# Feed-forward in plain float32 matmuls, with W2 as the stationary operand and a transposed accumulator

## The reference

```
a = layernorm(x)                       # over the channels, eps 1e-6
q, k, v = a @ Wq, a @ Wk, a @ Wv       # 8 heads of 16
s = q k^T / 4 + time_bias + particle_bias, -inf where the key's time is later
x = x + softmax(s) v @ Wo
t = layernorm(x)                       # eps 1e-5
p = softmax(t @ Wg); top two of 8, made to sum to 1: top0, top1
for i in 0, 1:
    w_in = t * top_i
    out += sum over all 8 experts e of gelu(w_in @ W1[e] + b1[e]) @ W2[e]  + sum(b2)
x = x + out
```

## Time and profile before

| | |
|---|---|
| median of 3 runs | 2823.3 us (2819.64 to 2824.63) |
| span of the profiled execution | 2817.5 us, 5.8 us below the median of the runs; the profile gives no other time for this execution |
| mean granted TensorE clock | 0.965 of full speed |
| TensorE busy | 2460.9 us, 87% |
| ScalarE busy | 1694.7 us, 60% |
| VectorE busy | 1485.6 us, 53% |
| GpSimd busy | 1087.3 us, 39% |

### The profile page before, as it was taken

One profiled execution on the slowest core, in us unless ns is written; L12 is line 12 of the kernel. 1 busy time (PEld: TensorE's weight loads), 2 busy tenths in 40 slices (PEclk: granted clock), 3 DMA queues, 4 the chain that ended last, 5 costly groups with the idle time before them and its releaser, 6 DMA issues.

```text
span 2817.5 us, 57193 instructions
## 1 busy us (share of the span) xinstructions
PE 2460.9 (87%) x18611; PEld 2132.1 (76%) x18611; DVE 1485.6 (53%) x4157; ACT 1694.7 (60%) x2788; POOL 1087.3 (39%) x1054
## 2 busy tenths in 40 slices
PE   1658989899998989989899898989989898998989
PEld 0447778787877878877787777878877787877879
DVE  7545375445636554474554636544573555547454
ACT  2126666665665666556566665666566566656667
POOL 6014244343424434343343424333343433434337
PEclk9679999999999999999999999999999999999999
DMA  2412121030212203021030212103021120302100
GB/s 32 71 37 29 22 33 27 10 47 10 27 27 30 29 7 49 6 32 27 12 46 9 29 25 32 27 8 48 10 27 27 25 35 7 43 11 32 27 9 7
DMA packets 62290, 73.55 MB, mean 26 GB/s; under 512 B 15936, under 2 KB 43488, under 8 KB 61920
## 3 DMA queue, kind: packets, MB, share of 16 engines
q1 hardware_dynamic: 62016, 69.89, 17.1%
HBM read 11.19 MB, written 6.29 MB: 6 GB/s over the span
## 4 chain that ended last, share of the span: by engine, by line
PE 65%; DVE 12%; issue 10%; ACT 8%; DMA 2%; POOL 1%; SPq 1%; DVEq 0%; POOLq 0%; ACTq 0%
PE acc L912 17%; PE zps L901 8%; PE wide L819 7%; PE narrow L852 5%; PE wide L835 5%; ACT z L512 5%; PE zps L902 5%; PE zps L903 5%; PE wide L838 4%; PE wide L866 2%; PE wide L873 2%; DVE wide L664 1%; DVE h L735 1%; PE wide L859 1%; DMA stack<-halves 1%
## 5 line engine op out<-in xcount | busy, mean ns | idle before, releaser
L453 POOL TENSOR_TENSOR hsum<-h 128x384 f32<-128x384 f32 x1024 | 1027.6, 1007 | 1575.0 <-ACT h L541 1507.3
L540 ACT ACTIVATE h<-zps,b_col 128x384 f32<-128x384 f32 x1024 | 594.2, 580 | 751.6 <-DVE h L735 728.3
L735 DVE TENSOR_TENSOR h<-zps,ratio_b 128x384 f32<-128x384 f32 x1024 | 562.1, 554 | 910.1 <-PE zps L903 906.1
L912 PE MATMUL acc<-w,hsum 128*128 128x128 f32 x6144 | 863.0, 277 | 1.4 <-DVE outt L744 1.2
L912 PEld LDWEIGHTS acc<-w,hsum 128*128 128x128 f32 x6144 | 845.8, 194 | 2.2 <-POOL hsum L453 1.7
L541 ACT ACTIVATE h<-h,b_col 128x384 f32<-128x384 f32 x1024 | 620.4, 606 | 0.0
L901 PE MATMUL zps<-x_hi,w_lo 128*128 128x384 f32 x1024 | 449.8, 439 | 105.8 <-ACT h L540 64.0
L664 DVE CUSTOM_DVE_ANT_0 wide<-wide,query_table 128x768 f32<-128x768 f32 (+5 forms) x768 | 463.0, 651 | 123.1 <-PE wide L819 117.3
L835 PE MATMUL wide<-stack 128*128 128x256 f32 (+3 forms) x1280 | 364.7, 317 | 71.8 <-ACT z L512 33.6
L512 ACT ACTIVATE z<-wide 128x896 f32<-128x896 f32 (+2 forms) x384 | 344.8, 918 | 87.3 <-PE wide L838 86.8
L902 PE MATMUL zps<-x_lo,w_hi 128*128 128x384 f32 x1024 | 352.5, 344 | 0.0
(11 more groups left out here) (110 smaller groups left out, 1611.8 us busy)
## 6 DMA issues: line engine op xcount, KB each, us to landing
stack<-halves SPq DMA_DIRECT2D x512, 96.0 KB, 3.6
x_in<-in_x SPq DMA_DIRECT2D x136, 48.0 KB, 2.4
out_dram<-outt SPq DMA_DIRECT2D x256, 24.0 KB, 1.6
z<-in_L_ffn_W SPq DMA_DIRECT2D x8, 256.0 KB, 4.2
stack<-max_rows SPq DMA_DIRECT2D x64, 12.0 KB
bias_rows<-w_hi SPq DMA_DIRECT2D x1, 192.0 KB
bias_rows<-w SPq DMA_DIRECT2D x1, 192.0 KB
bias_rows<-w_lo SPq DMA_DIRECT2D x1, 192.0 KB
```

The costliest lines, as they stand in the source:

```text
L453: pool.tensor_tensor(hsum[:, m % NHS, :], h0[:, m % 2, :], h1[:, m % NH1, :], ALU.add).then_inc(hsum_ready, 1)
L540: act.activation(h0[:, m % 2, :], zps[m % 2][:, 0:CT], ACT.Gelu, bias=b1_col[:, j:j + 1]).then_inc(h0_ready, 1)
L735: vec.tensor_tensor(h1[:, m % NH1, :], zps[m % 2][:, 0:CT], ratio_b[:, c * CT:(c + 1) * CT], ALU.mult).then_inc(z1_ready, 1)
L912: ins = pe.matmul(acc[:, n * P:(n + 1) * P], hsum[:, k % NHS, n * P:(n + 1) * P], w2[:, j, :], start=(j == 0 and n == 0), stop=(j == UNITS ...
```

## The change

Layer one: W1 and x0 are kept whole in float32 (`w1`, `x0`), and a unit is one plain float32 matmul over 384 columns. The rounding and subtracting of W1 and of x0 go away; W1 is loaded straight to its place, right behind W2, during the first batch's attention. `x0` and `ratio_b` are two halves of one tile, which ScalarE fills with one copy per chunk.

Layer two: the W2 block is stationary and `hsum` moves, 384 columns in one matmul. The accumulator is then channels by tokens and has to be turned back: at the end of a chunk VectorE copies it to `acc_t`, TensorE transposes its three tiles into the same bank, and VectorE adds the residual as before. For chunk 0 the copy is in slot 31 and the transposes and the add in slot 33, for chunk 1 all is in slot 63 (`FINISH`). There are two accumulator banks, one for each chunk.

The second accumulator takes the bank of `narrow`. `mix` now writes both its parts into one wide buffer, and ScalarE copies 768 columns once, at the second part. `gate` writes to the free columns of the wide buffer that `turn` used, which is held until VectorE has taken the gate's maxima.

```diff
+FINISH = (33, UNITS - 1)
-WIDE = {(s, a): n for n, (s, a) in enumerate([(s, a) for _, s, a in PLAN if s in WIDE_STEPS])}
+WIDE = {(s, a): n for n, (s, a) in enumerate([(s, a) for _, s, a in PLAN if s in WIDE_STEPS and (s != "mix" or a[1])])}
+WIDE.update({("mix", (g, 0)): WIDE["mix", (g, 1)] for g in range(GROUPS)})
...
-        x0_hi = sb("x0_hi", [P, TOK], F32R)
-        x0_lo = sb("x0_lo", [P, TOK], F32R)
-        ratio_b = sb("ratio_b", [P, TOK])
+        x0_ratio = sb("x0_ratio", [P, 2, TOK])
+        x0, ratio_b = x0_ratio[:, 0], x0_ratio[:, 1]
+        acc_t = sb("acc_t", [P, CT])
...
-        acc = ps("acc", [P, 512])
-        narrow = ps("narrow", [P, 512])
+        acc = [ps("acc0", [P, 512]), ps("acc1", [P, 512])]
...
 SyncE, prepare
-                elif (step, a) == ("mix", (1, 1)):
-                    sp.wait_ge(narrow_filled, NARROW["mix", (1, 1)] + 1)
-                    for a in range(2):
-                        for e in range(4):
-                            sp.dma_start(z[:, a, e * DFF:(e + 1) * DFF], W1[4 * a + e]).then_inc(w1_loaded, 16)
+                    for e in range(EXPERTS):
+                        sp.dma_start(w1[:, e, :], W1[e]).then_inc(w1_loaded, 16)
...
 ScalarE, mix
-                elif step == "mix":
-                    cols = QCOLS if qc == 0 else TOK - QCOLS
-                    act.copy(mixed[:, qc * QCOLS:qc * QCOLS + cols], narrow[:, 0:cols]).then_inc(narrow_free, 1)
+                elif step == "mix" and a[1] == 1:
+                    act.copy(mixed[:, :], w[:, 0:TOK]).then_inc(wide_free[s], 1)
...
 ScalarE, split
-                    act.copy(x0_hi[:, a * CT:(a + 1) * CT], w[:, 0:CT]).then_inc(split_high, 1)
-                    act.copy(ratio_b[:, a * CT:(a + 1) * CT], w[:, 512:512 + CT]).then_inc(split_high, 1)
+                    act.copy(x0_ratio[:, :, a * CT:(a + 1) * CT],
+                             w[:, :].rearrange("p (k t) -> p k t", k=2)[:, :, 0:CT]).then_inc(wide_free[s], 1)
...
 VectorE, split
-                    vec.wait_ge(split_high, r.at(4, 2 * a + 2))
-                    ins = vec.tensor_tensor(x0_lo[:, a * CT:(a + 1) * CT], w[:, 0:CT], x0_hi[:, a * CT:(a + 1) * CT],
-                                            ALU.subtract)
-                    ins.then_inc(wide_free[s], 1)
...
 VectorE, after
                     vec.wait_ge(hsum_used, r.at(UNITS, k + 1 + NHS))
+                    vec.tensor_copy(acc_t[:, :], acc[c][:, 0:CT]).then_inc(acc_copied, 1)
+                if k in FINISH:
+                    c = FINISH.index(k)
+                    vec.wait_ge(out_turned, r.at(CHUNKS, c + 1))
                     vec.wait_ge(out_stored, r.at(16 * TPT * CHUNKS, 16 * (TPT * c + 1)))
                     vec.wait_ge(res_ready, r.at(CHUNKS, CHUNKS))
-                    vec.tensor_tensor(outt[:, :, :], acc[:, 0:CT].rearrange("p (i c) -> p i c", c=C),
+                    vec.tensor_tensor(outt[:, :, :], acc[c][:, 0:CT].rearrange("p (i c) -> p i c", c=C),
                                       res[:, c * HT:(c + 1) * HT, :], ALU.add).then_inc(out_ready, 1)
...
 TensorE, unit
-                pe.matmul(zp, lo, x0_hi[:, cols], start=True, stop=False)
-                pe.matmul(zp, hi, x0_lo[:, cols], start=False, stop=False)
-                pe.matmul(zp, hi, x0_hi[:, cols], start=False, stop=True).then_inc(z_filled, 1)
+                pe.matmul(zps[m % 2][:, 0:CT], w1[:, e, t * P:(t + 1) * P], x0[:, cols], start=True,
+                          stop=True).then_inc(z_filled, 1)
...
 TensorE, after
-                for n in range(HT):
-                    ins = pe.matmul(acc[:, n * P:(n + 1) * P], hsum[:, k % NHS, n * P:(n + 1) * P], w2[:, j, :],
-                                    start=(j == 0 and n == 0), stop=(j == UNITS_PER_CHUNK - 1), skip_group_check=True)
-                ins.then_inc(hsum_used, 1)
+                pe.matmul(acc[c][:, 0:CT], w2[:, j, :], hsum[:, k % NHS, :], start=(j == 0),
+                          stop=(j == UNITS_PER_CHUNK - 1)).then_inc(hsum_used, 1)
+                if k in FINISH:
+                    c = FINISH.index(k)
+                    pe.wait_ge(acc_copied, r.at(CHUNKS, c + 1))
+                    for n in range(HT):
+                        ins = pe.transpose(acc[c][:, n * P:(n + 1) * P], acc_t[:, n * P:(n + 1) * P], ident[:, :])
+                    ins.then_inc(out_turned, 1)
```

More of the change, by code:

```diff
@@ L82 @@
 PLAN = attention_plan()
-WIDE_STEPS = ("turn", "query", "key", "value", "maxima", "rows", "scores", "sums", "divide", "project", "split")
-NARROW_STEPS = ("mix", "gate")
-WIDE = {(s, a): n for n, (s, a) in enumerate([(s, a) for _, s, a in PLAN if s in WIDE_STEPS])}
-NARROW = {(s, a): n for n, (s, a) in enumerate([(s, a) for _, s, a in PLAN if s in NARROW_STEPS])}
+WIDE_STEPS = ("turn", "query", "key", "value", "maxima", "rows", "scores", "mix", "sums", "divide", "project", "split")
+WIDE = {(s, a): n for n, (s, a) in enumerate([(s, a) for _, s, a in PLAN if s in WIDE_STEPS and (s != "mix" or a[1])])}
 assert len(WIDE) % 2 == 0
 WPB = len(WIDE) // 2
-NPB = len(NARROW)
+WIDE.update({("mix", (g, 0)): WIDE["mix", (g, 1)] for g in range(GROUPS)})
 VCHAIN = 2 * (5 + 3 * NEWTON) + 7
@@ L464, in prepare @@
                                        pattern=[[0, HEADS], [-PARTS, TPT], [0, PARTS]], channel_multiplier=1).then_inc(setup_done, 1)
[L465 to L469, removed]
-                        pool.tensor_tensor(w1_lo[:, 4 * a:4 * a + 4, :], z[:, a, 0:2048].rearrange("p (e f) -> p e f", f=DFF),
-                                           w1_hi[:, 4 * a:4 * a + 4, :], ALU.subtract).then_inc(w1_low, 1)
             rounds(pool, lambda r, step, a: None, unit, lambda r, k: None, prepare=prepare)
@@ L548, in prepare @@
                             act.copy(bias_hi[g][row:row + n], raw[g][row:row + n, :, :]).then_inc(bias_high, 1)
-                elif (step, a) == ("turn", 1):
-                    act.wait_ge(w1_loaded, 16 * 8)
-                    act.wait_ge(bias_placed, 16 * BIAS_DMAS)
-                    for a in range(2):
-                        act.copy(w1_hi[:, 4 * a:4 * a + 4, :], z[:, a, 0:2048].rearrange("p (e f) -> p e f", f=DFF)).then_inc(w1_high, 1)
             act.wait_ge(act_set, 2)
@@ L790, in attention @@
                         pe.wait_ge(wide_free[s], free)
-                if step in NARROW_STEPS:
-                    free = r.at(NPB, NARROW[step, a])
-                    if not (isinstance(free, int) and free <= 0):
-                        pe.wait_ge(narrow_free, free)
                 if step == "turn":
@@ L876, in attention @@
                 elif step == "gate":
-                    pe.wait_ge(*taken(r, "turn", 1))
+                    pe.wait_ge(turned, r.at(1, 1))
+                    w = wide[WIDE["turn", 1] % 2]
                     for i in range(TILES):
-                        ins = pe.matmul(narrow[:, i * EXPERTS:(i + 1) * EXPERTS], act_t[:, i * P:(i + 1) * P], wg[:, :],
+                        ins = pe.matmul(w[:, TOK + i * EXPERTS:TOK + (i + 1) * EXPERTS], act_t[:, i * P:(i + 1) * P], wg[:, :],
                                         start=True, stop=True)
-                    ins.then_inc(narrow_filled, 1)
+                    ins.then_inc(gate_filled, 1)
                 elif step == "split":
```

72 lines of the change are left out of this document (35 added, 37 removed).

## The result

The changed kernel takes 2935.34 us (median of 4 runs, 2934.95 to 2938.44) against 2822.1 us before: a ratio of 1.0402, 95% interval 1.0387 to 1.0416. It is 4.0% slower; 2928 us had been forecast, in a range of 2870 to 2985.

A forecast was written before the change was run, and what follows sets the result against it. TensorE was taken to bound 48 of a pass's 64 units and all of the last pass, a VectorE chain elsewhere. +6.5 us a pass times 15, plus +7.3 once, made +105 us: 2928 us, range 2870 to 2985.

The forecast's parts named there:

- The unit: Feed-forward unit, layers one and two on TensorE: grows from 1.20 to 1.29 us, +4.3 us a pass for 48 warm units.
- Rival E: Attention slots: VectorE sets the pace, so the unit's growth and the finishes hide; 2804 us, chance 0.04.
- Rival C: Feed-forward unit: long records carry the float32r extra, or it grows a whole pass; +0.06 us a unit, 2975 us, chance 0.10.
- the price by counting passes: Feed-forward unit: 8 array passes for 7, one more pass of 0.16 us a unit, some 50 us more in the sum.
- The end of chunk 1: Slot 63: TensorE waits for VectorE's copy, then makes three transposes before the loop's turn; +1.9 us a pass.
- Rival B: End of chunk 1 is hidden and the 16 units outside the warm slots cost nothing; about 2880 us, chance 0.12.
- The clock: After the loop's turn: three units a pass at the 1.2 GHz level cost 0.2 us more each, +0.6 us.
- rival D: Loop's end costs 3 us more, with more of the next pass at 1.2 GHz; 2973 us, chance 0.04.
- The split: Slot 60: one ScalarE copy of 768 columns lets the next batch's first unit start earlier; -1.3 us a pass.
- Chunk 0's finish, mix and gate: Slot 33: three transposes cost TensorE +0.35 us a pass; mix and gate in the wide buffers cost nothing.
- Once: Outside the repeated passes: last pass +7.3 us; before the first, gate -6.5 and W1's earlier load +6.5 cancel.

The follow-up runs named there:

- e5: Changed kernel with layer one over only the first 330 of a chunk's 384 columns; 2861.99 us, ratio 1.0144 to before.
- e3: Changed kernel with layer two of chunk 1 alone put back (hsum stationary, no copy or transposes there); 2885.21 us, ratio 1.0234 to before.
- e11: Changed kernel with chunk 1's accumulator copied by ScalarE, ahead of its next Gelu, in place of VectorE; 2919.11 us, ratio 1.0350 to before.
- e2: Changed kernel with layer two put back for both chunks (hsum stationary, no copies or transposes); 2895.78 us, ratio 1.0263 to before.
- e4: Changed kernel with the load of W1 moved back behind the first batch's last mix; 2930.01 us, ratio 1.0385 to before.
- e7: Changed kernel with layer one in three float32r passes and layer two of chunk 1 put back to hsum stationary; 2817.39 us, ratio 0.9988 to before.
- e9: e7 with three unused float32 matmuls over 384 columns just ahead of the loop's turn; 2801.09 us, ratio 0.9928 to before.
- e10: e9 with three more unused matmuls in the stall between the split's transposes and the first unit; 2796.65 us, ratio 0.9918 to before.
- e6: Changed kernel with twelve unused transposes while TensorE stands for VectorE's copy at the end of a pass; 2931.06 us, ratio 1.0390 to before.
- e1: Changed kernel with layer one put back to three float32r passes, W1 and x0 in halves, W1 loaded late; 2863.35 us, ratio 1.0150 to before.

## Why the prediction was right

The path was read rightly, TensorE in Q and the end of chunk 1 paid in full, and two terms were sized too low. Point by point, per pass, with what was measured:

- **The unit.** +0.09 forecast from L803's and L804's rows; 1.29 us measured, for 1.20. By the unit starts of e5 the 50 units of Q pay it in full (about 4.5 us; 4.3 forecast for 48), those at the end of a pass less than half: in P, 0.54 us for 14 slots, 0.04 each (0.65 forecast for 13). Rival E, VectorE's pace, fell with e5. Rival C, the extra of float32r on every long record, fell with the timeline: two records take 0.645 us. The four-pass rule of the Trainium skill (FP8 and Floating Point Precision, TensorE Precision Notes) agrees with this length (384 columns four times at 2.4 GHz are 0.640); the price by counting passes, 0.16 us a unit, does not agree, because the unit before took 1.20 us and not the 1.12 of seven bare passes.
- **The end of chunk 1.** +1.9 us forecast for P, 3.1 measured by e3. The order of the steps was right, and so was the wait (1.4 us) with the transposes. What I mis-sized is the turn: I took it as a constant behind TensorE's last work, and it is 2.5 us in the kernel before and 3.6 in the changed one, where the wait and the transposes stand just ahead of it. Rival B, a hidden end, fell with e3, and e11 confirms it from the other side.
- **The clock.** +0.6 us forecast, because three units on the 1.2 GHz level would grow by more. Mis-sized: around the turn, with a longer stand ahead of it, 2.9 instead of 1.7 us of full speed are lost. That is rival D's mechanism at less than half its price. In Q alone, where it costs time, the turn's loss is 2.2 instead of 1.5 us, and the first burst of scores adds 0.6, of which the prediction had nothing; the burst is 0.4 us longer by it. Around the split 0.5 us came back, which the prediction had only as a bound.
- **The split.** -1.3 us forecast. The idle time fell by 1.4 (2.75 to 1.34; no run prices it by itself), and VectorE's h starts right after its residual add, as worked out.
- **Chunk 0's finish, mix and gate.** +0.35 forecast for the finish, 0.33 measured by e2 against e3. For mix and gate nothing was forecast; e4 and e7 show no loss by them, and no run takes them out alone.
- **Once.** 6.4 us for W1 ahead of the maxima (bounds 0 to 9) and 6.5 back in the gate, forecast to cancel. Measured: +6.4, undone by e4 (7.9), and a first pass that gains 4.6 us in spite of its 64 longer units. Its gate is 6.5 us shorter, as forecast, and TensorE's wait for the first Gelus another 3.7 (8.4 to 4.6), which nothing in the prediction had. The Trainium skill (SBUF — State Buffer, Who interferes with whom) says that a VectorE instruction with both inputs in SBUF contends with a reading GpSimd. The trace agrees: with GpSimd's W1 subtraction beside it the gate's subtraction took 3.00 us, and takes 0.21 without. That GpSimd work is two instructions back to back:

```profile
198.84 9.14 POOL L470 TENSOR_TENSOR w_lo<-z,w_hi 128x2048 fp32r<-128x2048 f32 x2 [112.65 <-ACT w_hi L554]
```

  The first ends at 203.34 us and VectorE's L694 at 203.40; the second at 207.98 and L700 at 208.01. So each of the two VectorE instructions lasted until the GpSimd instruction beside it had ended, while a VectorE reduction and a reciprocal of 0.2 us, with one input each, ran between them, beside the second GpSimd instruction, at their usual length.

Summed by what was measured: P is 3.1 - 1.4 + 0.5 = +2.2 (measured 2.20; 1.25 forecast). Q, by the unit starts, is 4.5 from the units, about 0.5 more in the ten first units of a pass (the clock), 0.3 more in the first burst of scores and 0.3 for chunk 0's transposes, 5.6 in all (measured 5.67; 5.25 forecast). The forecast of 6.5 us a pass stands against 7.9: the end of the pass was sized too low by 1.2 us and the clock in Q by some 0.4. That the total is nearer, 105 us forecast and 113 measured, is in part luck: the sum counts all 15 passes as longer and lets only the gate stand against the W1 load, while the first pass came out 4.6 us shorter.

## What to carry to other kernels

Count a tensor engine's bill in passes times columns and read the price of each kind of pass from a row of the same kernel: fewer and longer instructions are not less work, and three float32r passes stayed below one float32 matmul here. A transposed accumulator is cheap only where its copy and its transposes have two slots of other work between them; the same finish just ahead of a loop's turn cost 3.1 us a pass, and in mid-pass 0.33. And where TensorE must stand, look at what clock it comes back with before shortening anything else.

## What the runs showed of the hardware

- Unused matmuls in a stall raised the speed. Three float32 matmuls over 384 columns just ahead of the turn cost P 0.2 us and gave Q 1.5 (e9); with three more at the split no clock was lost at either place (e10), and the kernel took 2796.65 us for 2817.39 without either, 0.7% less. Transposes placed ahead of a wait rather than in the turn itself gave Q 0.4, of it 0.24 behind the turn (e6).
- The turn of the hardware loop cost TensorE 2.3 to 2.6 us from its last work to the next pass when layer two's passes lay just ahead (before, e2, e3, e7), and 3.3 to 3.6 when a wait for the copy and three transposes did (the changed kernel, e1, e5, e6, e11). In e6, with twelve unused transposes in that wait, it was still 3.5. No run tells the reason.
- The clock fell in the first burst of scores in 5 of 14 passes of the changed kernel, in 12 of e5 and in none of e11, behind a stand of TensorE of 1.72 us in every pass of the changed kernel and of e11, and of 1.6 us in e5; a burst with a fall in it was 1.0 to 1.1 us longer.
- A small VectorE instruction with both inputs in SBUF lasted until the GpSimd subtraction beside it had ended, 3.00 and 3.83 us, within 0.06 us of its end both times.
- Eight loads of 256 KB took SyncE 8.5 us to issue behind another 2 MB load, where the kernel before had needed 3.7 for eight loads of the same size later on; the small transfer behind them landed in 6.0 instead of 2.9 us.
